# A decoder layer on one core: cross attention's exactness test summed on TensorE with one branch, and self-attention in another order

## The chip, the cores and the metric

The kernel runs on one core of one Trainium2 chip, as one program with nine stages one after the other. The metric is the time of one execution in device microseconds, taken as the median of three runs. A measurement of this kernel can tell about 0.2% (some 10 us) from no change.

## What is computed

The reference is one decoder layer over x of shape (4, 1024, 512), with a context of shape (4, 2048, 384). Cut to what matters here:

```python
x = _layernorm(x + attn(x))          # windows of 128 rows, stride 64
x = _layernorm(x + xattn(x, ctx))    # top 32 of 2048 keys per row and head
x = _layernorm(x + ffn(x))

# attn: softmax inside each window, windows that overlap are averaged, then @ Wo + bo
# xattn:
scores = einsum('bthd,bghd->bhtg', Q, K) / sqrt(DH)     # 4 heads
topv, topi = jax.lax.top_k(scores, 32)
attn = zeros.at[..., topi].set(softmax(topv)).mean(over heads)
c_t = attn @ V                                          # goes on to FiLM and a long convolution
```

## The kernel before

Both stages that the change touches go over 32 tiles of 128 rows (`TILES`), 8 tiles for each of the 4 batches (`TPB`). Each engine has its own program, written by hand; the engines meet only at semaphores, and an engine that waits holds up everything behind it in its own program. So the order of the lines in each engine's `tile` function is the schedule.

**Self-attention** (`stage_attention`, buffers `at_...`) is a software pipeline. In the step of tile i, TensorE multiplies the queries of tile i+1 with the folded weights (`queries`, L1022, into `ps_t`), turns the probabilities of tile i (L1055), turns the normalised rows of tile i-1 (`x1_turned`, L1038), mixes tile i (L1063), makes the cross-attention queries of tile i-1 (`cross_q`, L1045), the scores of tile i+1 (`scores`, L1031), turns the input of tile i+2 (`x_turned`, L1009), and projects tile i (L1075, into `ps_y`). VectorE computes a bias of the scores (`row_bias`, L1176, L1181), copies `ps_t` to `tT` (`queries_copied`, L1187), forms the low half of the cross queries (`q_lo`, L1218), does the softmax (L1194 to L1212), and then the residual and the layer norm of tile i: L1231 adds the input, L1233 adds the bias row, L1235 to L1239 the statistics, GpSimd the inverse root (L994), L1242 writes `x1`, which is printed as `at_x` in the rows. ScalarE copies the scores (L1100), the turned input (L1093), the mix (L1135) and the turned x1 (L1113), and does the exponentials (L1105 to L1107).

**Cross attention** (`stage_cross`, buffers `xa_...`) has to find the 32nd largest of 2048 scores of each row and head. `scan` (L1714) takes the 8 largest of each of 32 segments of 64 scores, `rank` (L1720 to L1729) the 32 largest of what is kept of these. That can miss a score, so `rank` ends with a test: four instructions (L1736), one a head, compare the kept candidates with the 32nd largest and sum the weighted hits of each row into `flag`. TensorE sums `flag` over the rows with a column of ones (`sum_flags`, L1573), VectorE casts the four sums to integers (L1786), and `settle` loads them into registers (L1746) and branches four times (L1748), once a head. A head whose sum is over 128 x 32 is searched again in full (L1751 to L1760). Then come the reciprocals and diagonals (L1772, L1777), and `select` (L1766) zeroes all exponentials below the 32nd score. In VectorE's step for tile t these pieces of tile t alternate with the scans of tile t+1: scan of head 0 in two parts with the cast between them, `settle`, scan of head 1, `diagonals`, `select` of heads 0 and 1, scan of head 2, `select` of heads 2 and 3, scan of head 3, `rank` of tile t+1.

TensorE's step for tile t: `sum_flags(t)`, scores of heads 1 and 2 of tile t+1 (L1566), the mix of tile t-1 (L80 to L82, 48 matmuls), the turns of tile t for the first half of the keys (`turn`, L1585) with the scores of head 3 of tile t+1 between them, the scores of head 0 of tile t+2, and the turns for the second half. All scores go through the same four PSUM banks, so each group waits for ScalarE's copy of the group before (L1629). ScalarE's step: copy of head 1, the split of the turned weights (`hi`, L1647 and L1650; GpSimd makes the low half, L1530), the denominators (L1634) and exponentials (L1640) with the copies of heads 2, 3 and 0 between them.

## Time and profile before

| | |
|---|---|
| median of 3 runs | 4885.35 us (4882.67 to 4885.68) |
| the profiled execution | 4882.0 us, its span 4880.3 us |
| busy share of the span | TensorE 83%, VectorE 55%, ScalarE 29%, GpSimd 27% |
| self-attention, first and last write of x1 | 532.3 and 986.6 us |
| cross attention, first and last sum of flags | 1131.2 and 2441.8 us |

The busy shares are means over nine stages with different limits; the change touches only the two stages in the last two lines of the table, some 10% and 28% of the span, so the rows below are taken from single steps inside them.

### The profile page before, as it was taken

What the parts mean: (1) busy time and instruction counts of PE and PEld (TensorE: products, weight loads), DVE (VectorE), ACT (ScalarE), POOL (GpSimd) and SP (SyncE); (2) the same over time, 40 slices, a digit from 0 to 9 for tenths busy, and PEclk for the clock granted to TensorE, in tenths of its full rate; (3) what the DMA queues carried; (4) which work ended last, traced back from release to release, by engine and by line L of the source; (5) the groups of instructions that cost most, each with busy time, mean ns of one, the idle gap of its engine ahead of it and who ended that gap; (6) DMA issues with size and microseconds to landing.
All of it is one profiled execution on the core that took longest, in us unless ns stands there. A gap on an engine that the chain in (4) does not pass through costs nothing. (4 is left out here: it accounts for less than half of the span.)

```text
span 4880.3 us, 63397 instructions
## 1 busy us (share of the span) xinstructions
PE 4037.1 (83%) x20652; PEld 3291.2 (67%) x20652; DVE 2698.5 (55%) x9097; ACT 1431.6 (29%) x2179; POOL 1299.0 (27%) x1123
## 2 busy tenths in 40 slices
PE   6845788865787875867779889795999999999998
PEld 4722677634776764757768767574887887887886
DVE  8644455518998989998945455422443446322222
ACT  2344233324555553445510010221211112111111
POOL 0000000001112120111136513102676775432332
PEclk8668999987888887888889989896999999999999
DMA  1144322252010110110034423433222223100000
GB/s 57 36 145 113 103 81 81 65 186 57 11 44 30 30 43 7 30 33 21 8 106 143 141 87 118 147 117 132 63 67 62 77 68 103 31 25 19 25 24 18
DMA packets 248556, 336.31 MB, mean 69 GB/s; under 512 B 67525, under 2 KB 125765, under 8 KB 245959
## 3 DMA queue, kind: packets, MB, share of 16 engines
q1 hardware_dynamic: 151976, 177.79, 12.2%
q10 hardware_dynamic: 93744, 146.84, 8.9%
q0 software_dynamic: 2560, 8.39, 0.4%
q8 instruction: 126, 2.06, 0.2%
q14 instruction: 150, 1.22, 0.1%
HBM read 220.70 MB, written 112.25 MB: 68 GB/s over the span
## 5 line engine op out<-in xcount | busy, mean ns | idle before, releaser
L1585 PE MATMUL xa_ps_t<-xa_diag,xa_s_buf 128*128 128x128 f32 x4096 | 499.4, 282 | 162.3 <-DVE xa_s_buf L1766 96.0
L1585 PEld LDWEIGHTS xa_ps_t<-xa_diag,xa_s_buf 128*128 128x128 f32 x4096 | 483.3, 197 | 192.4 <-DVE xa_s_buf L1766 113.4
L1714 DVE MAX8 xa_cand<-xa_s_buf 128x8 f32<-128x64 f32 x4096 | 534.9, 216 | 119.4 <-issue 58.0
L3011 DVE CAST m_act_hl<-m_g 128x512 fp32r<-128x512 f32 x256 | 137.4, 537 | 831.1 <-ACT m_g L2879 831.1
L2705 POOL TENSOR_TENSOR m_act_hl<-m_g,m_act_hl 128x512 fp32r<-128x512 f32 x256 | 355.8, 1390 | 659.1 <-DVE m_act_hl L3011 659.1
L2879 ACT ACTIVATE m_g<-m_ps_h,m_b 128x512 f32<-128x512 f32 x256 | 176.2, 688 | 1095.3 <-PE m_ps_h L82 1090.2
L1530 POOL TENSOR_TENSOR xa_aT<-xa_a,xa_aT 128x512 fp32r<-128x512 f32 x128 | 159.9, 1271 | 1004.0 <-ACT xa_a L1650 1004.0
L80 PE MATMUL m_ps_h<-m_hT,m_w 128*128 128x512 f32 x1024 | 413.6, 404 | 6.3 <-issue 4.3
L80 PE MATMUL m_ps_o<-m_w,m_act_hl 128*128 128x512 f32 x1024 | 406.9, 397 | 0.7 <-POOL m_act_hl L2705 0.7
L82 PE MATMUL m_ps_h<-m_hT,m_w 128*128 128x512 f32 x1024 | 406.4, 397 | 0.0
L82 PE MATMUL m_ps_o<-m_w,m_act_hl 128*128 128x512 f32 x1024 | 406.3, 397 | 0.0
L81 PE MATMUL m_ps_h<-m_hT,m_w 128*128 128x512 f32 x1024 | 406.2, 397 | 0.0
L81 PE MATMUL m_ps_o<-m_w,m_act_hl 128*128 128x512 f32 x1024 | 406.1, 397 | 0.0
L1629 ACT ACTIVATE xa_s_buf<-xa_ps_s 128x2048 f32<-128x2048 f32 x128 | 239.8, 1873 | 404.4 <-PE xa_ps_s L1566 329.4
L1766 DVE SCALAR_TENSOR_TENSOR xa_s_buf<-xa_s_buf,xa_top,xa_prob 128x2048 f32<-128x2048 f32 x128 | 294.6, 2344 | 4.5 <-ACT xa_prob L1640 0.8
L1566 PE MATMUL xa_ps_s<-xa_ks,xa_qs 128*128 128x512 f32 x512 | 190.0, 503 | 109.1 <-ACT xa_s_buf L1629 87.0
L1640 ACT ACTIVATE xa_prob<-xa_s_buf,xa_nmax 128x2048 f32<-128x2048 f32 x128 | 252.4, 2001 | 31.5 <-DVE xa_s_buf L1766 31.5
L80 PE MATMUL xa_ps_ac<-xa_ctx_hl,xa_aT 128*128 128x384 f32 x512 | 206.7, 404 | 48.1 <-POOL xa_aT L1530 48.1
L80 PEld LDWEIGHTS m_ps_h<-m_hT,m_w 128*128 128x128 f32 x1024 | 193.3, 189 | 55.9 <-issue 11.3
L80 PEld LDWEIGHTS m_ps_o<-m_w,m_act_hl 128*128 128x128 f32 x1024 | 193.2, 189 | 48.6 <-POOL m_act_hl L2705 2.0
L82 PEld LDWEIGHTS m_ps_o<-m_w,m_act_hl 128*128 128x128 f32 x1024 | 193.5, 189 | 46.9
L82 PEld LDWEIGHTS m_ps_h<-m_hT,m_w 128*128 128x128 f32 x1024 | 193.5, 189 | 46.9
(369 smaller groups left out, 8111.6 us busy)
## 6 DMA issues: line engine op xcount, KB each, us to landing
at_xk<-in_x_dram SPq DMA_DIRECT2D x128, 128.0 KB, 2.7
spectrum<-df_yo ACTq DMA_DIRECT2D x32, 512.0 KB, 2.8
id_raw<-spectrum SPq DMA_DIRECT2D x32, 512.0 KB, 6.1
m_xt<-x ACTq DMA_DIRECT2D x64, 256.0 KB, 4.0
ky_raw<-in_ctx_dram SPq DMA_DIRECT2D x16, 768.0 KB, 6.3
xa_ks<-kt SPq DMA_DIRECT2D x48, 256.0 KB
xa_raw<-in_ctx_dram SPq DMA_DIRECT2D x32, 384.0 KB, 3.4
w<-bf_out_t SPq DMA_DIRECT2D x32, 256.0 KB, 2.5
```

The costliest lines, as they stand in the source:

```text
L80: pe.matmul(out, w_hi, m_lo, start=start, stop=False)
L81: pe.matmul(out, w_lo, m_hi, start=False, stop=False)
L82: return pe.matmul(out, w_hi, m_hi, start=False, stop=stop)
L1530: pool.tensor_tensor(aT[:, 1, 4 * g:4 * g + 4, :], a32[:, g % 2, :, :], aT[:, 0, 4 * g:4 * g + 4, :].bitcast(F32), ALU.subtract).then_inc( ...
L1566: last = pe.matmul(ps_s[:, c, :], qs[:, t % 2, h, :], ks[:, h, c * 512:(c + 1) * 512], start=True, stop=True)
L1585: last = pe.matmul(ps_t[:, c // 4, c % 4, :], s_buf[:, t % 2, h, k0:k0 + P], diag[:, h, :], start=(h == 0 and c % 4 == 0), stop=(h == HEAD ...
L1629: act.activation(s_buf[:, t % 2, h, :], ps_s[:, :, :].rearrange("p c n -> p (c n)"), ACT.Copy).then_inc(s_sc, 1)
L1640: act.activation(prob[:, h % 2, :], s_buf[:, t % 2, h, :], ACT.Exp, bias=nmax[:, t % 2, h:h + 1], scale=SCALE).then_inc(s_exp, 1)
L1714: dve.max(out=ranks[h][:, :, g], in_=s_buf[:, t % 2, h, g * SEG:(g + 1) * SEG])
L1766: dve.scalar_tensor_tensor(out=s_buf[:, t % 2, h, :], in0=s_buf[:, t % 2, h, :], scalar=top[:, t % 2, h, TOPK - 1:TOPK], in1=prob[:, h % 2 ...
L2705: pool.tensor_tensor(lo, g32[:, :], hi.bitcast(F32), ALU.subtract).then_inc(s_gl, 1)
L2879: act.activation(g32[:, :], ps_h[:, n % 2, :], ACT.Gelu, bias=b1[:, cur, n:n + 1]).then_inc(s_g, 1)
```

## The change

In cross attention the four compares of a tile become one compare of all heads (L1777 of the changed kernel) that writes ones and zeros in bf16 over `cand_b`. TensorE sums them in two steps: `sum_rows`, eight matmuls whose moving operand `to_head` sends head h to column h and everything to column 4, then, after a copy by ScalarE (`row_sums`) and after the scores of head 1, `sum_flags`, two matmuls with the weights that the compare held before. `settle` loads only the sum over all heads and branches once; the four loads and four branches lie inside that branch. The cast of the sums now stands behind 24 of the 32 segments of the scan, where it stood behind 16. In self-attention the bias row and the input are added on GpSimd two tiles ahead (`xb`), which leaves VectorE one addition before the statistics; TensorE and ScalarE take the same work in another order, and VectorE copies `ps_t` before `row_bias` and does `q_lo` inside the softmax.

```diff
-                with pool.Fori(0, B) as b:
-                    for j in range(TPB):
-                        pool.wait_ge(s_var, b * TPB + j + 1)
-                        pool.tensor_tensor(rstd[:, :], mv[:, 1:2], neghalf[:, :], ALU.pow).then_inc(s_rstd, 1)
+                pool.wait_ge(s_w, 16 * 7)
+                pool.tensor_tensor(b_row[:, :], b_row[:, :], bo[:, :], ALU.add)
+                pool.drain()
+
+                def tile(b, j, first, last):
+                    i = b * TPB + j
+                    pool.wait_ge(s_var, i + 1)
+                    pool.tensor_tensor(rstd[:, :], mv[:, 1:2], neghalf[:, :], ALU.pow).then_inc(s_rstd, 1)
+                    if not (isinstance(b, int) and i + 2 >= TILES):
+                        bb, jj = after(b, j, 2)
+                        slot = jj % SLOTS
+                        pool.wait_ge(s_x[slot], 80 * (bb * (TPB // SLOTS) + jj // SLOTS + 1))
+                        pool.tensor_tensor(xb[:, jj % 2, :], xq[:, slot, :], b_row[:, :], ALU.add).then_inc(s_xb, 1)
+
+                for j in range(2):
+                    pool.wait_ge(s_x[j], 80)
+                    pool.tensor_tensor(xb[:, j, :], xq[:, j, :], b_row[:, :], ALU.add).then_inc(s_xb, 1)
+                batches(pool, tile)
...
-                def queries(b, j):
+                def queries(b, j, first, end):
 
                     k, i = j % 2, b * TPB + j
-                    pe.wait_ge(s_xTc, i + 1)
-                    pe.wait_ge(s_tc, i)
-                    if not (isinstance(i, int) and i < 3):
-                        pe.wait_ge(s_ql, i - 2)
-                    for m in range(DC):
+                    if first == 0:
+                        pe.wait_ge(s_xTc, i + 1)
+                        pe.wait_ge(s_tc, i)
+                    for m in range(first, end):
                         for c in range(DC):
                             last = pe.matmul(ps_t[:, m, :], m_qk[:, c, m * P:(m + 1) * P], xT[:, k, c, 64:64 + P],
                                              start=(c == 0), stop=(c == DC - 1))
-                    last.then_inc(s_t, 1)
+                    if end == DC:
+                        last.then_inc(s_t, 1)
...
-                        queries(*after(b, j, 1))
+                        queries(*after(b, j, 1), 0, DC - 1)
                     pe.wait_ge(s_att, i + 1)
                     pe.wait_ge(s_aTc, i)
                     for h in range(2):
                         done = pe.transpose(ps_s[:, (2 + h) * P:(3 + h) * P], att[:, h * P:(h + 1) * P], ident[:, :])
                     done.then_inc(s_aT, 1)
-                    if not first:
-                        x1_turned(i - 1, (j + 1) % 2)
+                    if not last:
+                        queries(*after(b, j, 1), DC - 1, DC)
                     pe.wait_ge(s_aTc, i + 1)
                     pe.wait_ge(s_oc, i)
                     for c in range(DC):
@@ -1064,11 +1080,13 @@
                                              start=(h == 0), stop=(h == 1))
                     done.then_inc(s_o, 1)
                     if not first:
-                        cross_q(i - 1)
+                        x1_turned(i - 1, (j + 1) % 2)
                     if not last:
                         scores(*after(b, j, 1))
-                        if not (isinstance(b, int) and i + 2 >= TILES):
-                            x_turned(*after(b, j, 2))
+                    if not first:
+                        cross_q(i - 1)
+                    if not last and not (isinstance(b, int) and i + 2 >= TILES):
+                        x_turned(*after(b, j, 2))
                     pe.wait_ge(s_oc, i + 1)
...
-                    if not first:
-                        x1_copied(i - 1)
                     act.wait_ge(s_o, i + 1)
                     act.wait_ge(s_y, i)
                     act.activation(oT[:, :, :], ps_o[:, :, :], ACT.Copy).then_inc(s_oc, 1)
                     if not first:
-
+                        x1_copied(i - 1)
+                    if not last:
+                        scores_copied(i + 1, 1 - k)
+                    if not first:
                         q_hi(i - 1, 1 - k, b * (TPB // 2) + (j - 1) // 2)
                     if not last:
-                        scores_copied(i + 1, 1 - k)
                         if not (isinstance(b, int) and i + 2 >= TILES):
                             x_copied(i + 2, k)
                         exponentials(i + 1, 1 - k)
...
-                def softmax(i, j):
+                def q_lo(i, k):
+                    dve.wait_ge(s_qh, i + 1)
+                    dve.tensor_tensor(qhl[:, k, 1, :], ps_c[:, P:2 * P], qhl[:, k, 0, :].bitcast(F32), ALU.subtract)\
+                       .then_inc(s_ql, 1)
+
+                def softmax(i, j, q, rounds):
 
                     k = j % 2
                     dve.wait_ge(s_sc, i + 1)
@@ -1195,6 +1215,8 @@
                     dve.tensor_reduce(mx[0:64, k, 1:2], sc[0:64, k, 0:P], AX.X, ALU.max, negate=True)
                     dve.tensor_reduce(mx[64:128, k, 1:2], sc[64:128, k, P:2 * P], AX.X, ALU.max, negate=True)
                     dve.drain().then_inc(s_mx, 1)
+                    if rounds:
+                        q_lo(q, j % 2)
...
                     if not last:
+                        queries_copied(i + 1, 1 - k)
                         row_bias(*after(b, j, 1))
-                        queries_copied(i + 1, 1 - k)
-                    if not first:
-                        q_lo(i - 1, 1 - k)
                     if not last:
-                        softmax(i + 1, (j + 1) % TPB)
+                        softmax(i + 1, (j + 1) % TPB, i - 1, not first)
                     dve.wait_ge(s_y, i + 1)
-                    dve.tensor_tensor(res[:, :], ps_y[:, :], xq[:, slot, :], ALU.add)
-                    dve.drain()
-                    dve.tensor_tensor(res[:, :], res[:, :], b_row[:, :], ALU.add)
+                    dve.wait_ge(s_xb, i + 1)
+                    dve.tensor_tensor(res[:, :], ps_y[:, :], xb[:, k, :], ALU.add)
                     dve.drain()
                     dve.bn_stats(stats[:, :], res[:, :])
...
-                pool.memset(ones[:, :], 1.0).then_inc(s_const, 1)
+                pool.memset(f_weight[:, :], 1.0)
+                pool.drain()
+                pool.affine_select(out=f_weight[:, 0:1], in_=f_weight[:, 0:1], compare_op=ALU.not_equal, fill=2.0,
+                                   base=-7, pattern=[[0, 1]], channel_multiplier=1)
+                pool.affine_select(out=f_weight[:, 1:2], in_=f_weight[:, 1:2], compare_op=ALU.is_ge, fill=0.0,
+                                   base=SEGS - NW, pattern=[[0, 1]], channel_multiplier=1)
+                pool.drain().then_inc(s_const, 1)
...
-                def sum_flags(t):
+                def sum_rows(t):
+
                     pe.wait_ge(s_cand, t + 1)
                     if t >= 1:
                         pe.wait_ge(s_chk, t)
-                    pe.matmul(ps_f[:, :], ones[:, :], flag[:, t % 2, :], start=True, stop=True).then_inc(s_f, 1)
+                    for a in range(2):
+                        for h in range(HEADS):
+                            last = pe.matmul(ps_f[0:NW, a, :], flags[:, h, a, :], to_head[:, h, :], start=(h == 0), stop=(h == HEADS - 1))
+                    last.then_inc(s_fr, 1)
+
+                def sum_flags(t):
+                    pe.wait_ge(s_frc, t + 1)
+                    for a in range(2):
+                        last = pe.matmul(ps_f[0:1, 2, :], f_weight[:, a:a + 1], f_sums[:, a, :], start=(a == 0), stop=(a == 1))
+                    last.then_inc(s_f, 1)
...
                 scores(1, 0)
                 for t in range(TILES):
+                    sum_rows(t)
+                    if t + 1 < TILES:
+                        scores(t + 1, 1)
                     sum_flags(t)
                     if t + 1 < TILES:
-                        scores(t + 1, 1)
                         scores(t + 1, 2)
...
+                def row_sums(t):
+                    act.wait_ge(s_fr, t + 1)
+                    act.activation(f_sums[:, :, :], ps_f[0:NW, 0:2, :], ACT.Copy).then_inc(s_frc, 1)
...
+                    row_sums(t)
                     if t + 1 < TILES:
                         copy(t + 1, 1)
...
-                    for h in range(HEADS):
-                        dve.scalar_tensor_tensor(out=junk[:, h, :, :],
-                                                 in0=cand[:, h, :].rearrange("p (a x) -> p a x", a=2)[:, :, 0:NW],
-                                                 scalar=top[:, k, h, TOPK - 1:TOPK], in1=f_weight[:, :, :],
-                                                 op0=ALU.is_ge, op1=ALU.mult, accum_out=flag[:, k, h:h + 1])
+                    dve.tensor_tensor(flags[:, :, :, :], cand[:, :, :].rearrange("p h (a x) -> p h a x", a=2)[:, :, :, 0:NW],
+                                      top[:, k, :, TOPK - 1:TOPK].rearrange("p h (a x) -> p h a x", a=1).broadcast_to([P, HEADS, 2, NW]),
+                                      ALU.is_ge)
                     dve.tensor_scalar(nmax[:, k, :], top[:, k, :, 0], -SCALE, None, ALU.mult)
                     dve.drain().then_inc(s_cand, 1)
 
                 def settle(t):
                     k = t % 2
                     left = prob[:, 0, :]
-                    doubts = [dve.value_load(flag_i[0:1, h:h + 1], min_val=0, max_val=P * NW * 4) for h in range(HEADS)]
-                    for h in range(HEADS):
-                        with dve.If(doubts[h] > P * TOPK):
-                            src = s_buf[:, k, h, :]
-                            for r in range(TOPK // 8):
-                                dve.max(out=top[:, k, h, 8 * r:8 * r + 8], in_=src)
+                    doubt = dve.value_load(flag_i[0:1, HEADS:HEADS + 1], min_val=0, max_val=P * NW * 4 * HEADS)
+                    with dve.If(doubt > P * TOPK * HEADS):
+                        doubts = [dve.value_load(flag_i[0:1, h:h + 1], min_val=0, max_val=P * NW * 4) for h in range(HEADS)]
+                        for h in range(HEADS):
+                            with dve.If(doubts[h] > P * TOPK):
+                                src = s_buf[:, k, h, :]
...
-                        scan(t + 1, 0, 0, 16)
+                        scan(t + 1, 0, 0, 24)
                     if t >= 0:
                         dve.wait_ge(s_f, t + 1)
-                        dve.tensor_copy(flag_i[:, :], ps_f[:, :])
+                        dve.tensor_copy(flag_i[:, :], ps_f[0:1, 2, :])
                         dve.drain()
                     if more:
-                        scan(t + 1, 0, 16, SEGS)
+                        scan(t + 1, 0, 24, SEGS)
```

TensorE's program for one step of self-attention before, from one group of query matmuls to the next (`at_ps_x<-at_ident,at_x` are the turns of x1 of the tile before; `at_ps_x<-at_ident,at_xk` those of the input):

```order
L1022 MATMUL at_ps_t<-at_xT,at_m_qk 128x128 x16
L1055 MATMUL at_ps_s<-at_ident,at_att 128x128 x2
L1038 MATMUL at_ps_x<-at_ident,at_x 128x128 x4
L1063 MATMUL at_ps_o<-at_attT,at_xk 128x128 x8
L1045 MATMUL at_ps_c<-at_x1T,at_wxq 128x128 x4
L1031 MATMUL at_ps_s<-at_xT,at_tT 128x256 x4
L1009 MATMUL at_ps_x<-at_ident,at_xk 128x128 x8
L1075 MATMUL at_ps_y<-at_w_vo,at_oT 128x512 x4
```

The same step in the changed kernel:

```order
L1037 MATMUL at_ps_t<-at_xT,at_m_qk 128x128 x12
L1071 MATMUL at_ps_s<-at_ident,at_att 128x128 x2
L1037 MATMUL at_ps_t<-at_xT,at_m_qk 128x128 x4
L1079 MATMUL at_ps_o<-at_attT,at_xk 128x128 x8
L1054 MATMUL at_ps_x<-at_ident,at_x 128x128 x4
L1047 MATMUL at_ps_s<-at_xT,at_tT 128x256 x4
L1061 MATMUL at_ps_c<-at_x1T,at_wxq 128x128 x4
L1025 MATMUL at_ps_x<-at_ident,at_xk 128x128 x8
L1093 MATMUL at_ps_y<-at_w_vo,at_oT 128x512 x4
```

A quarter of the query matmuls has moved behind the turns of the probabilities, the turns of x1 have moved behind the mix, and the scores stand ahead of the cross queries. The matmuls themselves are the same 50.

VectorE's program in cross attention before, from the end of `rank` to the first loads of `settle` (the load and its two register instructions come four times, then four branches):

```order
L1736 SCALAR_TENSOR_TENSOR xa_cand_b,xa_flag<-xa_cand,xa_top,xa_f_weight 128x208 x4
L1740 TENSOR_SCALAR xa_nmax<-xa_top 128x4
L1714 MAX xa_cand<-xa_s_buf 128x8 x16
L1786 CAST xa_flag_i<-xa_ps_f 1x4
L1714 MAX xa_cand<-xa_s_buf 128x8 x16
L1746 TENSOR_LOAD xa_flag_i
L1746 ISA x2
```

The same place in the changed kernel:

```order
L1777 TENSOR_TENSOR xa_cand_b<-xa_cand,xa_top 128x832
L1780 TENSOR_SCALAR xa_nmax<-xa_top 128x4
L1756 MAX xa_cand<-xa_s_buf 128x8 x24
L1828 CAST xa_flag_i<-xa_ps_f 1x5
L1756 MAX xa_cand<-xa_s_buf 128x8 x8
L1786 TENSOR_LOAD xa_flag_i
L1786 ISA x2
L1787 COMPARE_AND_BRANCH
L1788 TENSOR_LOAD xa_flag_i
```

One load and one branch stand between the scan of head 0 and that of head 1, behind eight segments of scan instead of sixteen; the next load is already inside the branch.

## Rows read from the trace of the kernel before

**Rows 1.** Stretches: length, busy PE, PEld, DVE, ACT, POOL, then granted clock, DMA, GB/s.
```profile
544.80:930.80 386.00, 343.85 (x2251) 281.08 (x2250) 198.65 (x656) 124.71 (x339) 14.81 (x27) 1.00 0.26 80
1217.50:1488.80 271.30, 214.67 (x1311) 194.19 (x1312) 248.25 (x1338) 147.67 (x178) 42.82 (x32) 0.86 0.11 30
...
1621.49:1624.50 3.01, 3.01 (x9) 3.01 (x10) 3.01 (x26) 3.01 (x10) 0.00 (x0) 0.51 0.00 0
```

**Rows 2.** TensorE's timeline, a self-attention step: start, duration in us; idle before in brackets.
```profile
704.04 3.73 PE L1022 MATMUL at_ps_t<-at_xT,at_m_qk 128*128 128x128 f32 x32
...
709.57 0.66 PE L1038 MATMUL at_ps_x<-at_ident,at_x 128*128 128x128 f32 x4 [1.58 <-DVE at_x L1242]
...
711.85 1.06 PE L1045 MATMUL at_ps_c<-at_x1T,at_wxq 128*128 128x128 f32 x8
712.74 1.89 PE L1031 MATMUL at_ps_s<-at_xT,at_tT 128*128 128x256 f32 x8
714.47 1.04 PE L1009 MATMUL at_ps_x<-at_ident,at_xk 128*128 128x128 f32 x8
...
718.78 0.38 PE L1022 MATMUL at_ps_t<-at_xT,at_m_qk 128*128 128x128 f32 x2
```

**Rows 3.** Waits of self-attention, 515 to 985 us: total, times, longest.
```profile
PE at_ps_x L1038 <- DVE at_x L1242: 50.5, 31, 3.6
```

**Rows 4.** Timeline of ScalarE and VectorE in the same step.
```profile
715.55 1.09 ACT L1093 ACTIVATE at_xT<-at_ps_x 128x512 f32<-128x512 f32 x2 [0.40 <-PE at_ps_x L1009]
...
720.23 0.69 DVE L1231 TENSOR_TENSOR at_res<-at_ps_y,at_xq 128x512 f32<-128x512 f32 x1
721.00 0.69 DVE L1233 TENSOR_TENSOR at_res<-at_res,at_b_row 128x512 f32<-128x512 f32 x1
...
723.61 0.55 DVE L1242 TENSOR_SCALAR at_x<-at_res,at_mv,at_rstd 128x512 f32<-128x512 f32 x1 [0.66 <-POOL at_rstd L994]
724.07 0.68 DVE L1176 SCALAR_TENSOR_TENSOR at_dot<-at_xq,at_u_q 128x512 f32<-128x512 f32 x1
...
725.09 1.12 DVE L1187 TENSOR_SCALAR at_tT<-at_ps_t,at_u_k 128x128 f32<-128x128 f32 x4
```

**Rows 5.** Timeline of VectorE over one tile of cross attention.
```profile
1614.42 0.16 DVE L1740 TENSOR_SCALAR xa_nmax<-xa_top 128x4 f32<-128x4 f32 x1
...
1616.95 2.13 DVE L1714 MAX8 xa_cand<-xa_s_buf 128x8 f32<-128x64 f32 x16
1621.31 4.16 DVE L1714 MAX8 xa_cand<-xa_s_buf 128x8 f32<-128x64 f32 x32 [2.23 <-issue]
...
1639.80 4.15 DVE L1714 MAX8 xa_cand<-xa_s_buf 128x8 f32<-128x64 f32 x32
...
1651.81 0.43 DVE L1736 SCALAR_TENSOR_TENSOR xa_cand_b<-xa_cand,xa_top,xa_f_weight 128x208 bf16<-128x208 f32 x1
...
1653.24 0.16 DVE L1740 TENSOR_SCALAR xa_nmax<-xa_top 128x4 f32<-128x4 f32 x1
```

**Rows 6.** VectorE's sequencer in `settle` of that tile: ns minimum/median/maximum, first and last start.
```profile
L1746 DVEq TENSOR_LOAD <-xa_flag_i x4: 297/300/310, 1617.6 to 1619.4; - x4
...
L1748 DVEq COMPARE_BRANCH  x4: 56/56/77, 1620.1 to 1621.0; - x4
```

**Rows 7.** Timeline of TensorE and ScalarE in the same tile.
```profile
1614.79 1.19 PE L1566 MATMUL xa_ps_s<-xa_ks,xa_qs 128*128 128x512 f32 x4
...
1621.49 0.69 PE L80 MATMUL xa_ps_ac<-xa_ctx_hl,xa_aT 128*128 128x384 f32 x1 [1.48 <-POOL xa_aT L1530]
...
1636.07 1.88 ACT L1629 ACTIVATE xa_s_buf<-xa_ps_s 128x2048 f32<-128x2048 f32 x1 [2.35 <-PE xa_ps_s L1566]
```

**Rows 8.** The full search's last addition: ns minimum/median/maximum, first and last start.
```profile
L1760 DVE TENSOR_TENSOR xa_s_buf<-xa_s_buf,xa_prob x3: 2291/2293/2293, 1882.1 to 2084.1; 128x2048 f32<-128x2048 f32 x3
```

**Rows 9.** Timelines of GpSimd: constants at cross attention's start, and one later pair.
```profile
1093.57 0.29 POOL L1524 TENSOR_SCALAR_AFFINE_SELECT xa_ident<-xa_ident 128x128 f32<-128x128 f32 x1 [0.41 <-issue]
...
1618.95 2.49 POOL L1530 TENSOR_TENSOR xa_aT<-xa_a,xa_aT 128x512 fp32r<-128x512 f32 x2 [12.09 <-ACT xa_a L1650]
```

More of the change, by code:

```diff
@@ L1078, in _ @@
                 x_turned(0, 0)
-                queries(0, 0)
+                queries(0, 0, 0, DC)
                 scores(0, 0)
@@ L1169, in _ @@
                     dve.memset(w[64:128, TPB - 1:TPB], val)
-                dve.tensor_tensor(b_row[:, :], b_row[:, :], bo[:, :], ALU.add)
-                dve.drain()
                 def row_bias(b, j):
@@ L1214, in softmax @@
                     dve.drain().then_inc(s_att, 1)
-                def q_lo(i, k):
-                    dve.wait_ge(s_qh, i + 1)
-                    dve.tensor_tensor(qhl[:, k, 1, :], ps_c[:, P:2 * P], qhl[:, k, 0, :].bitcast(F32), ALU.subtract)\
-                       .then_inc(s_ql, 1)
                 def tile(b, j, first, last):
@@ L1246, in _ @@
                 queries_copied(0, 0)
-                softmax(0, 0)
+                softmax(0, 0, None, False)
                 batches(dve, tile)
+                q_lo(TILES - 2, 0)
                 q_lo(TILES - 1, 1)
@@ L1412, in stage_cross @@
         qs = sb("qs", [P, 2, HEADS, P], F32R)
-        ones = sb("ones", [P, 1])
         s_buf = sb("s_buf", [P, 2, HEADS, S2])
@@ L1419, in stage_cross @@
         top = sb("top", [P, 2, HEADS, TOPK])
[L1420 to L1422 removed]
+        to_head = sb("to_head", [P, HEADS, HEADS + 1], BF16)
+        f_weight = sb("f_weight", [NW, 2])
+        f_sums = sb("f_sums", [NW, 2, HEADS + 1])
+        flag_i = sb("flag_i", [1, HEADS + 1], mybir.dt.int32)
         nmax = sb("nmax", [P, 2, HEADS])
@@ L1445, in stage_cross @@
         s_cand = sem("row_flags_done")
+        s_fr = sem("flags_summed_over_rows")
+        s_frc = sem("row_sums_copied")
         s_f = sem("flags_summed")
@@ L1458, in stage_cross @@
         s_st = [sem(f"mix_stored{k}") for k in range(2)]
+        flags = cand_b[:, :, :].rearrange("p h n -> p (h n)").bitcast(BF16).rearrange("p (h a x) -> p h a x", h=HEADS, a=2)
         with nc.Block() as block:
@@ L1745, in settle @@
                     left = prob[:, 0, :]
-                    doubts = [dve.value_load(flag_i[0:1, h:h + 1], min_val=0, max_val=P * NW * 4) for h in range(HEADS)]
-                    for h in range(HEADS):
-                        with dve.If(doubts[h] > P * TOPK):
-                            src = s_buf[:, k, h, :]
-                            for r in range(TOPK // 8):
-                                dve.max(out=top[:, k, h, 8 * r:8 * r + 8], in_=src)
+                    doubt = dve.value_load(flag_i[0:1, HEADS:HEADS + 1], min_val=0, max_val=P * NW * 4 * HEADS)
+                    with dve.If(doubt > P * TOPK * HEADS):
+                        doubts = [dve.value_load(flag_i[0:1, h:h + 1], min_val=0, max_val=P * NW * 4) for h in range(HEADS)]
+                        for h in range(HEADS):
+                            with dve.If(doubts[h] > P * TOPK):
+                                src = s_buf[:, k, h, :]
+                                for r in range(TOPK // 8):
+                                    dve.max(out=top[:, k, h, 8 * r:8 * r + 8], in_=src)
+                                    dve.drain()
+                                    dve.match_replace(out=left, in_to_replace=top[:, k, h, 8 * r:8 * r + 8], in_values=src,
+                                                      imm_value=TAKEN)
+                                    dve.drain()
+                                    src = left
+                                dve.tensor_scalar(left, left, 0.5 * TAKEN, -2.0 * BIG, ALU.is_ge, ALU.mult)
                                 dve.drain()
-                                dve.match_replace(out=left, in_to_replace=top[:, k, h, 8 * r:8 * r + 8], in_values=src,
-                                                  imm_value=TAKEN)
+                                dve.tensor_tensor(s_buf[:, k, h, :], s_buf[:, k, h, :], left, ALU.add)
                                 dve.drain()
-                                src = left
-                            dve.tensor_scalar(left, left, 0.5 * TAKEN, -2.0 * BIG, ALU.is_ge, ALU.mult)
-                            dve.drain()
-                            dve.tensor_tensor(s_buf[:, k, h, :], s_buf[:, k, h, :], left, ALU.add)
-                            dve.drain()
                     dve.drain().then_inc(s_chk, 1)
```

16 lines of the change are left out of this document (6 added, 10 removed).

## The prediction

> **What bounds the kernel now.** The page says that TensorE is busy most of the time, but that is a mean over nine stages, so I read the two touched stages alone. The table of stretches gives both [rows 1]: in the middle of self-attention TensorE is busy 344 of 386 us, VectorE 199; in one batch of cross attention VectorE is busy 248 of 271 us, TensorE 215. So the first stage is TensorE's, the second VectorE's, and each gain has to be found on that engine.
>
> In self-attention TensorE's timeline shows a step of 14.74 us with one hole: 1.58 us before the turns of x1, which wait for VectorE's L1242 [rows 2]. Everything behind is dense. The list of waits sums this hole to 50.5 us over 31 tiles; the longest, 3.6, belongs to the last [rows 3].
>
> In cross attention I take VectorE's timeline of one tile and count from the start of L1740 at 1614.42, which I call n. The next L1740 stands at 1653.24, so a tile takes 38.82 us; a batch has seven such periods, 271.30 / 7 = 38.76 [rows 1, 5]. VectorE's only large hole in it is 2.23 us ahead of the scan of head 1, put down to "issue" [rows 5]. The sequencer's rows say what that is: four loads 0.6 us apart (1617.6 to 1619.4), then four branches (1620.1 to 1621.0) [rows 6]. The scan ahead of them ends at 1616.95 + 2.13 = 1619.08, so part of the loads is hidden behind it and the rest is the hole.
>
> **Self-attention.** The matmuls stay the same. What is new is that the turns of x1 stand behind the mix, 2.7 us later than before in TensorE's order, while x1 comes earlier. TensorE alone then needs 14.74 - 1.63 = 13.1 us a tile (50.5 / 31 = 1.63). That holds only if the chain through VectorE, which decides when the next scores can start, is shorter. I add it up from the start of the scores in the new order: scores and cross queries 714.47 - 711.85 = 2.62; turns of the input until ScalarE takes them up 715.55 - 714.47 = 1.08; copies, exponentials and the softmax until the residual 720.23 - 715.55 = 4.68; from the only addition left to the start of x1 723.61 - 721.00 = 2.61; x1 until the next instruction 0.46; the copies to tT, now directly behind, 1.12 [rows 2, 4]. Handovers cost 0.04 (714.47 + 1.04 against 715.55). The sum is 12.6, 0.5 below 13.1: TensorE stays the bound and the whole hole goes. `q_lo` falls into the wait for the exponentials, `row_bias` behind tT, where nothing needs it until the scores are copied.
>
> The addition that leaves VectorE costs GpSimd one instruction of 128x512 a tile, 2.49 / 2 = 1.25 us [rows 9]; GpSimd is busy 14.81 of 386 us there [rows 1] and makes the row two tiles ahead, so it is late for nobody. It runs just behind the inverse root, beside L1242 and the copies to tT. Below, this costs nothing; above, it slows them by all of its 1.25 us, the chain becomes 13.9 and the gain 50.5 - 31 x 0.75 = 27. I take nothing, because these two read one tensor each and have 0.5 us of slack. The last tile keeps some of its 3.6 us, but saves a late addition (0.77, 721.00 - 720.23); the term is **50 us**, between 27 and 54.
>
> **Cross attention, VectorE's side.** The four compares run from 1651.81 to 1653.24, 1.43 us [rows 5]. The one that replaces them covers 832 elements. An addition of 512 took 0.69 [rows 4], one of 2048 2.29 [rows 8]: 1.04 ns an element and 0.16 to start, so 1.02, and the next starts a little before its end; I take 0.95. Bounds: 1.43 (no gain, should the bf16 output or the repeated operand be slow) and 0.86. Gain 0.48.
>
> `settle` now has one load and one branch behind eight segments (8 x 0.13 = 1.1 us). Its load begins at most 0.65 us after these (1617.6 - 1616.95, when sixteen were ahead of it), lasts 0.6, and the branch takes between a quarter and all of the 1.2 us from 1620.1 to 1621.31. So the hole is 0.65 + 0.6 + 0.3 + 0.1 - 1.1 = 0.6 us, with 0 and 1.5 as bounds. Gain 1.6. The scan of head 3, at 1639.80 or n + 25.4, could then start at n + 23.75.
>
> The Trainium skill ("Runtime: NRT & Kernel Launch", section "Instruction fetch mechanics") gives about 200 ns for a register load; by that three loads fewer would save 0.6 us, not 1.8. The trace has 0.6 apart, and the sum goes by it.
>
> **Cross attention, the other side.** The sums now take three engines. TensorE's eight matmuls, instead of one, start with the flags; ScalarE copies; after the scores of head 1 come two more. These scores began at n + 0.37 and took 1.19 [rows 7]; with `sum_rows` ahead they end near n + 2.2, and the sums lie ready at n + 2.5. The cast stands behind 24 segments, at n + 3.4: no wait, 0.9 us of slack.
>
> But everything on TensorE and ScalarE now starts `sum_rows` later: copy of head 1, split, GpSimd's low half, mix, turns, scores of head 3 and their copy, which ended at 1636.07 + 1.88 = n + 23.53 [rows 7] and releases the scan of head 3. Before, VectorE came 1.85 us after that. `sum_rows` is bounded by a matmul pass of self-attention, 3.73 / 32 = 0.12 [rows 2], so 0.95 for eight, less the old sum; below by 0.3. I take 0.6. The copy ends at n + 24.15, after VectorE is free: this chain is the new bound, and takes 0.4 of VectorE's gain. The period is 24.15 + (1651.81 - 1639.80) + 0.95 = 37.1, a gain of 1.7.
>
> Of 31 periods I count 25. The four after a batch's first tile hang on the context copies on ScalarE, behind which `row_sums` now stands: nothing gained, by choice (between -4 and +7 in all). Two contain full searches, three heads by [rows 8]; there a load and a branch are added, about 1 us. GpSimd's constants at the start become longer by two selects (0.29, after 0.41 of waiting [rows 9]), about 1 us, and the last tile has its `settle` unhidden and saves some 2. Together nothing. The term is 25 x 1.7 = **42 us**.
>
> **Sum.** 50 + 42 = 92 us. From the profiled execution's 4882.0 that is 4790, from the median of 4885.35, 3.35 higher, 4793. I predict 4792.
>
> **Rivals.**
> *The branch eats the load's gain* (10%). The single jump skips the code of all four heads. If it costs what keeps the hole at 2.2, VectorE comes to head 3 at n + 25.4 again, only the compare is gained, 25 x 0.48 = 12, and the time is 4882 - 62 = 4820 to 4823. For it: the first of four branches may already be dearer than the rest; against: they skip the same code now.
> *TensorE's clock rises* (12%). From 1621.49 to 1624.50 the granted clock is 0.51, that is 1.2 GHz, and the mix's first nine matmuls take twice their time [rows 1]; before that TensorE had waited 1.48 us [rows 7]. The added matmuls shorten its idle time. At 2.4 GHz the copy of head 3 comes 1.4 us sooner, VectorE bounds again at n + 23.75, and 25 x 0.4 = 10 us more are gained: 4782; with no hole left in `settle`, 4767.
> *GpSimd disturbs VectorE, or the chain of 12.6 is longer than I add* (10%): 27 instead of 50, 4815.
> *The outer branch is taken in every tile* (2%), if the sum of all heads never equals its bound. Then a load and a branch are added, 0.9 us against 0.48: 4882 - 50 + 31 x 0.4 = 4845. Against it: sums of ones and twos are exact.
> *Slower* (3%). A jump that has to wait for its code. It decides once it outweighs self-attention's 50 us and 10 more: 60 / 31 = 1.9 a tile on top of 38.8, so head 3 at 40.75 - 12.96 = n + 27.8 and a hole of 4.65 us, twice today's. The Trainium skill, in the section named above, says that a taken branch whose target is outside the current two pages stalls for a DMA fetch; four taken branches in 0.9 us [rows 6] show no such stall here, and the new target is where the fourth branch leads now.
>
> **How the numbers follow.** The forecast has 58%, with 4775 to 4808 as its own range; 5% lies between the cases. The range 4768 to 4825 takes in the clock, the branch and GpSimd and leaves out about 15%. Measurement tells 0.2%, some 10 us: faster 95%, same 2%, slower 3%.
>
> **What the changed profile would show.** Right: no wait of TensorE on L1256 (x1) in self-attention except at the end, and a step of 13.1 us; in cross attention steps of 37.1, under 1 us "issue" ahead of the scan of head 1, no wait of the cast, and a wait of the scan of head 3 for ScalarE's copy of about 0.4 us. Wrong: a new wait of the scores for tT, a hole of 2 us or more at `settle`, or a cast that waits for TensorE.

## The result, and the profile after

The changed kernel takes 4847.62 us (median of 4 runs, 4845.11 to 4848.71), the one before 4884.01 beside it: ratio 0.9924, 95% interval 0.9911 to 0.9938. The gain is 36 us where I had forecast 92, and the time lies outside my range.

The profiled span falls from 4880.3 to 4847.1 us. Cut at the first and the last instruction of each stage, self-attention goes from 506.1 to 473.1 us (-33.0), cross attention from 1399.5 to 1375.2 (-24.3), every stage but the last that the change doesn't touch by less than 1.5, and the last stage, the two MLPs, in which no line changed, from 1552.8 to 1576.1 (+23.3). So both gains are smaller than forecast, and a loss that I had not looked for takes back nearly all of the second.

Two stretches of the changed kernel, 24 steps of self-attention and seven tiles of cross attention; columns as in [rows 1]:

```profile
544.60:875.60 331.00, 320.72 (x2066) 261.08 (x2065) 187.56 (x577) 114.35 (x312) 42.78 (x49) 1.00 0.28 86
1178.82:1444.41 265.59, 214.31 (x1378) 195.60 (x1379) 246.54 (x1289) 147.95 (x185) 42.16 (x32) 0.84 0.11 31
```

A step is 331.00 / 24 = 13.79 us instead of 13.1, and TensorE still has holes. Its timeline, and the list of waits of the stage, show the new one, which answers to the hole of [rows 2, 3]:

```profile
683.62 0.66 PE L1054 MATMUL at_ps_x<-at_ident,at_x 128*128 128x128 f32 x4
684.68 1.99 PE L1047 MATMUL at_ps_s<-at_xT,at_tT 128*128 128x256 f32 x8 [0.41 <-DVEq L1203]
...
698.43 0.48 PE L1047 MATMUL at_ps_s<-at_xT,at_tT 128*128 128x256 f32 x1 [0.40 <-DVEq L1203]
```

```profile
PEld at_ps_s L1047 <- DVEq L1203: 20.7, 31, 1.4
```

The turns of x1 follow the mix without a gap, but the scores wait for tT. Why tT is late shows on GpSimd and VectorE (timelines of two steps; [rows 4] has the same line before, at 0.55 us):

```profile
682.01 1.27 POOL L1005 TENSOR_TENSOR at_xb<-at_xq,at_b_row 128x512 f32<-128x512 f32 x1
682.08 1.48 DVE L1256 TENSOR_SCALAR at_x<-at_res,at_mv,at_rstd 128x512 f32<-128x512 f32 x1 [0.66 <-POOL at_rstd L1000]
683.49 1.11 DVE L1202 TENSOR_SCALAR at_tT<-at_ps_t,at_u_k 128x128 f32<-128x128 f32 x4
...
693.23 0.69 DVE L1247 TENSOR_TENSOR at_res<-at_ps_y,at_xb 128x512 f32<-128x512 f32 x1 [0.19 <-issue]
...
695.77 1.26 POOL L1005 TENSOR_TENSOR at_xb<-at_xq,at_b_row 128x512 f32<-128x512 f32 x1
695.93 1.38 DVE L1256 TENSOR_SCALAR at_x<-at_res,at_mv,at_rstd 128x512 f32<-128x512 f32 x1 [0.76 <-POOL at_rstd L1000]
697.24 1.11 DVE L1202 TENSOR_SCALAR at_tT<-at_ps_t,at_u_k 128x128 f32<-128x128 f32 x4
```

The same operation takes 1.48 and 1.38 us instead of 0.55, and both times it ends 0.28 us after GpSimd's has ended (683.28 and 683.56, 697.03 and 697.31); so it is in all 30 tiles in which the two overlap (0.28 to 0.29).

In cross attention, VectorE's timeline of a tile that begins at n = 1567.33 answers to [rows 5]:

```profile
1566.39 1.03 DVE L1777 TENSOR_TENSOR xa_cand_b<-xa_cand,xa_top 128x832 bf16<-128x832 f32 x1
1567.33 0.16 DVE L1780 TENSOR_SCALAR xa_nmax<-xa_top 128x4 f32<-128x4 f32 x1
...
1570.67 0.13 DVE L1828 CAST xa_flag_i<-xa_ps_f 1x5 int32<-1x5 f32 x1
1570.88 1.12 DVE L1756 MAX8 xa_cand<-xa_s_buf 128x8 f32<-128x64 f32 x8
1572.41 4.16 DVE L1756 MAX8 xa_cand<-xa_s_buf 128x8 f32<-128x64 f32 x32 [0.41 <-issue]
...
1591.97 4.16 DVE L1756 MAX8 xa_cand<-xa_s_buf 128x8 f32<-128x64 f32 x32 [1.07 <-ACT xa_s_buf L1667]
...
1604.94 0.16 DVE L1780 TENSOR_SCALAR xa_nmax<-xa_top 128x4 f32<-128x4 f32 x1
```

The hole at `settle` is 0.41 us (forecast 0.6) and the compare takes 0.94 to the next instruction (0.95). But the tile lasts 37.61 instead of 37.1, because VectorE waits 1.07 us for the copy of head 3. TensorE and ScalarE in the same tile, as in [rows 7]:

```profile
1567.58 0.55 PE L1602 MATMUL xa_ps_f<-xa_to_head,xa_cand_b 128*104 128x5 bf16 x8 [1.96 <-DVEq L1781]
1567.99 1.25 PE L1592 MATMUL xa_ps_s<-xa_ks,xa_qs 128*128 128x512 f32 x4
...
1574.77 0.69 PE L80 MATMUL xa_ps_ac<-xa_ctx_hl,xa_aT 128*128 128x384 f32 x1 [1.48 <-POOL xa_aT L1556]
...
1590.06 1.88 ACT L1667 ACTIVATE xa_s_buf<-xa_ps_s 128x2048 f32<-128x2048 f32 x1 [4.03 <-PE xa_ps_s L1592]
```

The mix starts at n + 7.44 instead of 7.07, and the copy ends at n + 24.61 instead of the 23.53 that I started from.

In the last stage TensorE runs two loops of three passes each. Its timeline at the first jump back, of the kernel before and then of the changed one:

```profile
3672.00 0.49 PE L80 MATMUL m_ps_h<-m_hT,m_w 128*128 128x512 f32 x1 [0.64 <-issue]
```

```profile
3619.84 0.50 PE L80 MATMUL m_ps_h<-m_hT,m_w 128*128 128x512 f32 x1 [3.86 <-issue]
```

The sequencer's rows of the second loop, before and after (ns minimum/median/maximum; the minimum is the last pass, which doesn't jump):

```profile
L2558 PEldq COMPARE_BRANCH  x3: 83/215/215, 4408.8 to 4777.0; - x3
```

```profile
L2600 PEldq COMPARE_BRANCH  x3: 83/3517/3827, 4364.3 to 4743.2; - x3
```

The jump takes 3.5 us instead of 0.2. In its second pass (3616 to 3804.86 us) the first loop has this line in the list of DMA queues: queue, packets, MB, share of 16 engines.

```profile
q8 instruction: 9, 0.15, 0.3%
```

That queue carries instructions, in packets of 16 KB. In the same pass before (3672.00 to 3855.45 us) it moved none: now the loop's code is fetched anew. And behind the 3.9 us in which TensorE stands still, it goes on at half its clock for a while; the 4 us behind the jump, before and after (columns as in [rows 1]; 17 products against 11, at a granted clock of 1.00 and 0.57):

```profile
3672.00:3676.00 4.00, 4.00 (x17) 3.27 (x18) 1.42 (x5) 0.69 (x1) 0.55 (x1) 1.00 0.00 0
```

```profile
3619.84:3623.84 4.00, 4.00 (x11) 3.17 (x12) 0.00 (x0) 0.00 (x0) 0.00 (x0) 0.57 0.02 4
```

From the first jump of a loop to its second TensorE takes 188.9 us (3615.98 to 3804.86) instead of 184.1 (3671.36 to 3855.45), 4.8 more; four jumps make 19 of the 23.3.

### The profile page after: what moved, and what is told of

It is laid out like the page before. It is cut to its first block and busy times, and to the rows that moved or that the text cites. A ratio compares the mean times of both kernels' runs of the same rounds, so it can differ in the third digit from the quotient of the medians.

```text
span 4847.1 us, 63484 instructions
## 1 busy us (share of the span) xinstructions
PE 4054.5 (84%) x20972; PEld 3313.9 (68%) x20972; DVE 2695.3 (56%) x8842; ACT 1434.8 (30%) x2211; POOL 1338.0 (28%) x1158
## 5 line engine op out<-in xcount | busy, mean ns | idle before, releaser
L80 PE MATMUL m_ps_h<-m_hT,m_w 128*128 128x512 f32 x1024 | 416.9, 407 | 19.8 <-issue 17.8
L80 PEld LDWEIGHTS m_ps_h<-m_hT,m_w 128*128 128x128 f32 x1024 | 195.2, 191 | 70.0 <-issue 24.8
L82 PEld LDWEIGHTS m_ps_h<-m_hT,m_w 128*128 128x128 f32 x1024 | 195.2, 191 | 47.6
L80 PEld LDWEIGHTS m_ps_o<-m_w,m_act_hl 128*128 128x128 f32 x1024 | 193.5, 189 | 48.9 <-POOL m_act_hl L2747 2.0
L81 PEld LDWEIGHTS m_ps_h<-m_hT,m_w 128*128 128x128 f32 x1024 | 196.0, 191 | 43.9
```

The source lines that it names most:

```text
L80: pe.matmul(out, w_hi, m_lo, start=start, stop=False)
L81: pe.matmul(out, w_lo, m_hi, start=False, stop=False)
L82: return pe.matmul(out, w_hi, m_hi, start=False, stop=stop)
```

## The experiments

My theory after the result had three separate causes: GpSimd's addition beside VectorE's last operation; the chain over TensorE and ScalarE in cross attention, lengthened by `sum_rows` and by a low clock; and the place of the last stage's loops in the instruction stream, in front of which the change puts 636 TensorE instructions. The rivals are in the expectations. Of the kernels below, those without a word on it start from the changed kernel.

**The place of the loops.** Empty instructions at the start of TensorE's last stage, where it waits 28 us for a DMA in any case:

```diff
+                for _ in range(170):        # 60, 316; 124 in the kernel before
+                    pe.drain()
                 pe.wait_ge(s_const, 1)
                 pe.wait_ge(s_c, 16 * 7)
                 bias_products(0)
```

> The changed kernel with 170 empty TensorE instructions (drains) ahead of the last stage, in a stretch in which TensorE waits for weights anyway. Theory (place in the code): the change put more TensorE instructions ahead of the last stage's two loops, so that a loop now reaches over one fetch packet more than before and is fetched anew after each jump back; with 170 more, counted modulo 256 (a packet of 16384 bytes is 256 instructions of 64 bytes), both loops lie as favourably as before: the gap at the four jumps goes back from 3.9 us to about 0.6, instruction packets of the last stage from 62 to about 29, the stage from 1576 to about 1553 us, the kernel from 4847.6 to about 4825 us. Rival (the last stage is slower through something else, the clock or the memory): the gap and the time stay, 4847 to 4856 us.

Measured 4823.60 us; the last stage 1555.1, so that 21 of its 23.3 us are gone. The jump is back to its old length:

```profile
L2600 PEldq COMPARE_BRANCH  x3: 76/207/211, 4348.9 to 4717.1; - x3
```

> The same with 60 empty instructions instead of 170. Theory (place in the code): the loops' first instructions stay in the unfavourable half of a packet, so the gaps of 3.9 us and the refetching stay: 4847 us within 4, and the last stage within 3 us of 1576. Rival (empty instructions by themselves, or any shift, change the last stage): a time like that of the run with 170.

Measured 4846.39; the last stage 1575.7.

> The kernel before, nothing of the change in it, with 124 empty TensorE instructions ahead of the last stage (the changed kernel has about 636 more ahead of it, which is 2 packets of 256 and 124). Theory (place in the code): the last stage is lengthened as in the changed kernel: gaps of 3.9 us at the four jumps back, 1553 to about 1575 us, the kernel 4884 to about 4906. Rival (the new operations or their neighbours do it): no change, 4884 within 4.

Measured 4904.69, ratio 1.0042 (1.0028 to 1.0056); the last stage 1575.1. The old kernel becomes 20 us slower by 124 instructions that do nothing.

> The changed kernel with 316 empty TensorE instructions ahead of the last stage, which is 256 more than the 60 that changed nothing. Theory (the place counts modulo 256, a fetch packet): as with 60, gaps of 3.9 us at the four jumps, last stage 1576, 4847 within 4. Rival (enough empty instructions give TensorE's fetching a lead, and 170 were enough): last stage 1555, 4824.

Measured 4851.99; the last stage 1581.4, the waits for issue at the jumps as with 60 instructions (18.2 and 17.8 us in all). It is 5 us over the expected time: here the empty instructions themselves outlast the wait for the DMA, and the stage's first products wait 31.7 us for issue instead of 28.3 for the DMA. 170 empty instructions repair it, 60 and 316 don't: what counts is the place, not the head start.

**GpSimd beside VectorE.** Its addition for tile i+1 is issued behind the maxima of that tile, ahead of the inverse root, so that it falls into VectorE's wait for the exponentials:

```diff
                 def tile(b, j, first, last):
                     i = b * TPB + j
+                    if not last:
+                        bb, jj = after(b, j, 1)
...
+                        pool.wait_ge(s_mx, i + 2)
+                        pool.tensor_tensor(xb[:, jj % 2, :], xq[:, slot, :], b_row[:, :], ALU.add).then_inc(s_xb, 1)
                     pool.wait_ge(s_var, i + 1)
                     pool.tensor_tensor(rstd[:, :], mv[:, 1:2], neghalf[:, :], ALU.pow).then_inc(s_rstd, 1)
-                    if not (isinstance(b, int) and i + 2 >= TILES):
-                        bb, jj = after(b, j, 2)
...
```

> The changed kernel, with GpSimd's sum of the next tile's input and bias moved: it waits for the next tile's maxima, and so runs while VectorE waits for exponentials, and not beside VectorE's last operation of a tile. TensorE's program is the same. Theory (GpSimd slows VectorE): that last operation goes back from 1.48 to 0.55 us, TensorE no longer waits for the copied queries, the self-attention step goes from 13.79 to 13.0 or 13.1 us, the kernel from 4847.6 to about 4824. Rival (that operation is longer for another reason, its operands or its place): it stays at 1.48 us, and the time at 4847 within 5. Second rival (the operation shortens and something else holds the step): the step stays above 13.5, 4835 to 4847.

Measured 4821.58; self-attention 448.1 us. In the timelines the operation is back at 0.55, and in the stretch of 26 steps TensorE is busy throughout (337.09 / 26 = 12.97 us a step):

```profile
690.63 1.27 POOL L1004 TENSOR_TENSOR at_xb<-at_xq,at_b_row 128x512 f32<-128x512 f32 x1 [5.24 <-DVEq L1217]
...
698.71 0.55 DVE L1256 TENSOR_SCALAR at_x<-at_res,at_mv,at_rstd 128x512 f32<-128x512 f32 x1 [0.66 <-POOL at_rstd L1006]
```

```profile
543.07:880.16 337.09, 336.99 (x2238) 281.48 (x2237) 179.84 (x624) 121.49 (x338) 47.19 (x52) 1.00 0.29 92
```

The next kernel leaves the addition where it was, but makes it wait for the end of VectorE's operation:

```diff
+                        pool.wait_ge(s_x1, i + 1)
                         pool.tensor_tensor(xb[:, jj % 2, :], xq[:, slot, :], b_row[:, :], ALU.add).then_inc(s_xb, 1)
```

> The changed kernel, with GpSimd's sum of input and bias made to wait until VectorE has ended its last operation of the tile, so that it runs beside the four copies of the queries (one input, from PSUM) and the start of the row bias (two inputs, from SBUF). Theory (GpSimd slows only VectorE operations that read SBUF, by which kind is open): the last operation goes back from 1.48 to 0.55 us, the copies stay at 0.34, the step falls to 13.0 or 13.1 us; if the row bias is slowed it is by less than 0.9 us and hidden; 4822 to 4830. Rival (GpSimd slows whatever runs beside it by the same 0.9 us): the copies take 2 us instead of 1.1, the queries are as late as now, step 13.8, 4847 within 5.

Measured 4817.84, 4 us under the expected range; self-attention 448.3. The timelines of one step:

```profile
700.07 0.55 DVE L1257 TENSOR_SCALAR at_x<-at_res,at_mv,at_rstd 128x512 f32<-128x512 f32 x1 [0.66 <-POOL at_rstd L1000]
700.53 1.12 DVE L1203 TENSOR_SCALAR at_tT<-at_ps_t,at_u_k 128x128 f32<-128x128 f32 x4
701.78 0.80 DVE L1192 SCALAR_TENSOR_TENSOR at_dot<-at_xq,at_u_q 128x512 f32<-128x512 f32 x1
...
700.76 1.27 POOL L1006 TENSOR_TENSOR at_xb<-at_xq,at_b_row 128x512 f32<-128x512 f32 x1 [0.73 <-DVE at_x L1257]
```

The four copies from PSUM run beside GpSimd at their old 1.12 us. The row bias, which reads two rows from SBUF, overlaps GpSimd's last 0.25 us and takes 0.80 instead of 0.69. The rival, that anything beside GpSimd is slowed by the same 0.9 us, falls.

**The chain in cross attention.** First the order alone:

```diff
-                    sum_rows(t)
                     if t + 1 < TILES:
                         scores(t + 1, 1)
+                    sum_rows(t)
                     sum_flags(t)
...
-                    row_sums(t)
                     if t + 1 < TILES:
                         copy(t + 1, 1)
+                    row_sums(t)
```

> The changed kernel with the scores and the copy of the next tile's head 1 put ahead of the flags' first sum and of its copy, on TensorE and on ScalarE; the number of instructions is the same. Theory (the chain over TensorE and ScalarE ends the tile, since the sum of the flags delays the scores and the clock stays low longer): both engines idle for about 2 us before the flags, so the copies and the products come about 2 us earlier, the copy of head 3 ends before VectorE's other work does, VectorE no longer waits for it (1.07 us a tile), the period goes from 37.58 to about 36.5 us and the kernel from 4847.6 to about 4822. Rival (VectorE waits at that place for something else): period 37.6, no change, 4847 within 5.

Measured 4816.06; cross attention 1341.0 us, most tiles 36.45. VectorE's wait for the copies, in the changed kernel and then in this one (total, times, longest):

```profile
DVE xa_cand L1756 <- ACT xa_s_buf L1667: 67.4, 40, 18.7
```

```profile
DVE xa_cand L1756 <- ACT xa_s_buf L1667: 29.2, 8, 18.6
```

Then the one branch without `sum_rows`: the old compares and flag sum, and four products of one column for the total, behind the scores:

```diff
+                    pe.matmul(ps_f[:, 0:HEADS], ones[:, :], flag[:, t % 2, :], start=True, stop=True)
...
+                    for h in range(HEADS):
+                        last = pe.matmul(ps_f[:, HEADS:HEADS + 1], ones[:, :], flag[:, t % 2, h:h + 1],
+                                         start=(h == 0), stop=(h == HEADS - 1))
```

> The changed kernel with the old four compares and the old flag sum in cross attention, but with the one branch: the total is four more products of one column on TensorE, behind the scores of the next tile's head 1. TensorE has 128 instructions fewer in cross attention, so the last stage's loops should lie as before the change (22 us less in that stage). Theory (the sum over rows delays the scores and keeps the clock low): without it VectorE gains the jumps' 1.82 us a tile in full, period 38.75 - 1.82 = 36.9 us, less than the 37.58 of the whole change though VectorE does 0.5 us more; with 25 such tiles the kernel comes to about 4809. Rival (the products run longer at the low clock whatever sums the flags, because VectorE's tile is shorter): period about 37.5, 4825.

Measured 4833.11, and most tiles 37.8 to 38.1 us (37.1 to 40.2 in all): my theory missed, and the rival too. VectorE's timeline of a usual tile, from n = 1535.81:

```profile
1535.81 0.17 DVE L1765 TENSOR_SCALAR xa_nmax<-xa_top 128x4 f32<-128x4 f32 x1
...
1540.90 4.16 DVE L1739 MAX8 xa_cand<-xa_s_buf 128x8 f32<-128x64 f32 x32 [0.42 <-issue]
...
1560.13 4.16 DVE L1739 MAX8 xa_cand<-xa_s_buf 128x8 f32<-128x64 f32 x32 [0.73 <-ACT xa_s_buf L1655]
```

Without `sum_rows` the copy of head 3 is nearly as late as with it: by the median over 25 tiles (all but the last, the four after a batch's first, and the two with full searches) it ends at n + 24.29 against 24.58 in the changed kernel. So the chain had been longer than I thought before anything was added. The kernel before shows it when all its tiles are read instead of one: in the same 25 tiles that copy ended between n + 23.52 and n + 25.80, median 24.41. The tile of [rows 5, 7] is as early as any. Another one, ScalarE's copy and VectorE's start of the tile in the timeline:

```profile
1372.24 0.16 DVE L1740 TENSOR_SCALAR xa_nmax<-xa_top 128x4 f32<-128x4 f32 x1
...
1395.34 1.88 ACT L1629 ACTIVATE xa_s_buf<-xa_ps_s 128x2048 f32<-128x2048 f32 x1 [3.86 <-PE xa_ps_s L1566]
```

It ends at n + 24.98. The copy's end follows the number of the mix's 48 products that run at half clock: of the tiles whose mix began at n + 7.07 to n + 7.11, those with 9 such products ended the copy at n + 23.52 to 23.65, those with 15 at 24.41 to 24.49, those with 19 at 24.97 and 24.98. Before, it was 9 to 19 products (median 15), in the changed kernel 9 to 18 (median 13): the low clock, which I had blamed on the change, is no longer than before.

With that read, the branch alone with the scores put first should be VectorE's again:

> The four old compares and the old flag sum with the one branch, and the scores and the copy of the next tile's head 1 ahead of the flag sum. Theory (in the run with the branch alone the chain over TensorE and ScalarE ended the tile at 24.1 us, 0.4 to 0.5 us behind VectorE): with the scores earlier VectorE ends the tile, and the period is the 38.75 of before less the jumps' 1.82: 36.9 us, which is 0.5 more than the 36.46 with the single compare; the last stage lies favourably: 4806 within 5. Rival (the chain still ends the tile): 37.8, 4830.

Measured 4808.21; undisturbed tiles 36.93 (median of the 25 tiles 36.98). Beside `scores_first`'s 36.45 this gives the single compare by itself: 0.48 us a tile.

**The parts alone, and everything together.** The kernel before with one changed stage each:

> The kernel before, with the changed self-attention alone. TensorE's instructions ahead of the last stage are 4 fewer. Theory (three separate causes): self-attention 506 to 473 us, cross attention and the last stage as before: 4884 - 33 = about 4851. Rival (the parts act on each other, or self-attention too moves the last stage): the last stage at 1575, 4873.

Measured 4849.44, ratio 0.9936 (0.9920 to 0.9953); self-attention 473.5, cross attention 1397.2, the last stage 1555.2.

> The kernel before, with the changed cross attention alone: 640 TensorE instructions more ahead of the last stage. Theory: cross attention gives 24 us and the last stage takes 22 to 23 of them back through where its loops now lie, so that this half of the change moves the time by nearly nothing: 4879 to 4886. Rival (the last stage is slower only with both halves): about 4860.

Measured 4882.06, ratio 0.9997 (0.9988 to 1.0007); the same stages 506.4, 1374.6, 1575.7. This half of the change gains nothing on the whole, though it takes 25 us off its own stage.

> The changed kernel with three things at once: GpSimd's sum waits for the maxima, the scores and the copy of head 1 stand ahead of the flags' sum, and 170 empty TensorE instructions stand ahead of the last stage. Theory (three separate causes, in three stages): the gains add up, 26 from self-attention (4847.6 to 4821.6 by itself), about 25 from cross attention and 24 from the last stage: 4773 within 5. Rival (two of them share a cause, or the wait moves on): 4785 or more.

Measured 4768.84 us, ratio 0.9758 (0.9742 to 0.9775): 79 us less than the changed kernel, about the sum of the three single gains (26, 32 and 24). The three causes are separate.

## Why the prediction was wrong

**Self-attention, 50 us forecast, 33 measured.** TensorE's own need was right: 13.1 forecast, 12.97 when nothing else disturbs. The failing step is "I take nothing, because these two read one tensor each and have 0.5 us of slack": I had the upper bound right beside it, 13.9 us a step, and it is 13.79. Reading one tensor was no protection for the operation that writes x1. The slack was hardly there either. From the scores at 684.68 to those at 698.43 the chain takes 8.55 us until the residual at 693.23 (8.42 by my terms), 2.70 until x1 (2.61), 1.31 for x1 (0.46) and 1.19 from the copies to tT until the scores (1.12). With x1 undisturbed that makes 12.9 instead of 12.6, level with TensorE's 12.97.

The Trainium skill ("SBUF — State Buffer", section "Who interferes with whom") names `tensor_scalar` among the operations that can enter a 2-port mode, and says that such an operation and GpSimd exclude each other, the one that starts second being blocked until the first is through. The traces agree that the one that starts second waits: started 0.07 and 0.16 us behind GpSimd's 1.27 us, the operation ended 0.28 us behind its end both times. But a whole operation, 0.55 us, was not left by then, and no row shows which part of it had been done. That it was in such a mode no row says outright, but 512 elements took 0.55 us where an addition of 512 takes 0.69 [rows 4].

The rival "GpSimd disturbs VectorE, or the chain of 12.6 is longer than I add" had this cause, 27 us, and 10%.

**Cross attention, 42 forecast, 24 measured.** VectorE's side was right: hole 0.41 (0.6), compare 0.94 (0.95, and 0.48 gained), ready for head 3 at 1591.97 - 1.07 = n + 23.57 (23.75). In the two tiles shown `sum_rows` delays the mix by 0.37, less than my 0.6. The failing step is the chain's start: I took n + 23.53 for the end of the copy from one tile, the earliest. With the median, 24.41 + 0.37 gives n + 24.8 and a period of 37.7; the medians are n + 24.58 and 37.6. In the kernel before the chain's scatter cost little, because VectorE came at n + 25.4 and hid most of it; as the bound it shows. So the 25 tiles gave 28 us, not 42. What I had put "together" at nothing lost 4: behind the last `rank` alone the stage takes 48.7 us instead of 44.0 (45.7 and 45.3 in the two other kernels with the old stage). What lengthens that end was not tested. The cast waits only in the four tiles after a batch's first and in the last one; the four are no longer than before (46.0 to 47.8 us against 47.0 to 48.3).

**The last stage, 0 forecast, +23 measured.** The failing step is a term that was left out: the sum had this stage at nothing, without a word. I had asked what a jump's code costs on VectorE, where the change has its branch, and not what 636 more TensorE instructions do to jumps that come later. A pass of those loops is 1665 TensorE instructions.

The Trainium skill ("Runtime: NRT & Kernel Launch", section "Instruction fetch mechanics") gives blocks of 256 instructions, a store of 2048 for TensorE, and a stall where a jump's target is not in the current two pages. The blocks agree with the packets of 16 KB in that a shift by 256 instructions changes nothing (60 and 316); of the two pages the trace says otherwise, since before the change a jump back over 1665 instructions took 0.2 us. By those blocks a pass is 6.5 packets long and lies over seven or eight; my reading is that seven stay and eight are fetched anew.

Shown is that the jump's length hangs on the number of empty instructions ahead, up and down and in both kernels. All 14 kernels fit the reading: counted to the first jump and taken modulo 256, TensorE's instructions are 177 to 219 in the six whose jumps take 0.2 us, and 49 to 109 in the eight whose jumps take 3.3 to 3.9. The exact limit was not searched.

Of the rivals, the branch ate nothing (a hole of 0.41 us), and the clock did not rise (0.84 in the stretch of cross attention, 0.86 before). A jump that waits for its code came true, in another stage and on another engine than I had it.

## What to carry to other kernels

Before an engine's slack is counted, read the end of its chain in all tiles: a chain that is hidden today scatters unseen, and becomes the bound with its median, not with its best tile. An operation moved to GpSimd is priced by what VectorE does in the same microsecond; here it cost 25 us beside one operation, and nothing ahead of it or behind it. After a change, compare the stages that it does not touch too: where an engine has loops, the number of its instructions ahead can take back nearly all that half a change gains, and some empty ones in an idle stretch show it.

## What was not expected of the hardware

- A jump back on TensorE took 0.2 us or 3.3 to 3.9 us, by where the loop lay in the instruction stream; with the half clock behind it, 4.8 us a jump.
- Of the VectorE operations beside GpSimd's addition, 1.27 us long, a `tensor_scalar` from and to SBUF went from 0.55 to 1.48 us, a product of two rows in SBUF from 0.69 to 0.80 with 0.25 us of overlap, and copies out of PSUM kept their 1.12 us.
